# Self attention of a decoder kernel: low parts of the output weights and of the second half's key weights moved from VectorE to GpSimd

## The chip, the cores and the metric

One core of one Trainium2 chip runs the whole kernel. The metric is the device time of one execution in microseconds (us). The engines named below are TensorE (PE), VectorE (DVE), ScalarE (ACT), GpSimd (POOL) and SyncE (SP), which issues the DMAs.

## What is computed

The reference is a decoder of two layers over x of shape (16, 112, 512). Each layer is self attention, attention to a context, and a feed-forward part. The change touches only the second of these six parts, the attention of layer 0 with 16 query heads, 8 key heads and a head width of 128. It works on 16 sequences of 112 positions:

```python
b, s, _ = hidden_states.shape
ln_out = _ln(hidden_states, ln_w, ln_b)
q = _fp8_linear_pertensor(ln_out, wq, wq_scale, q_in_scale).reshape(b, s, g, hpg, d)
q = _ln(q, qln_w, qln_b)
k = _fp8_linear_pertensor(ln_out, wk, wk_scale, k_in_scale).reshape(b, s, g, d)
k = _ln(k, kln_w, kln_b)
v = _fp8_linear_pertensor(ln_out, wv, wv_scale, v_in_scale).reshape(b, s, g, d)
core = _gqa(q, k, v).reshape(b, s, nh * d)
...
cat = jnp.concatenate([core, xout], axis=-1)
catq = _div_clamp_fp8(cat, proj_smooth)
return jnp.einsum('bsi,oi->bso', catq, wproj) * (proj_in_scale * proj_w_scale)
```

The kernel keeps every weight matrix as the sum of two matrices of a reduced 32-bit format (fp32r): a high part, which is the scaled weight rounded, and a low part, which is the scaled weight minus the high part. A product with a weight is then two matmuls.

## The kernel before

`normed_attention` (L615) runs twice, once for self attention (`own` is true) and once for the context. Its work is cut into 32 steps (`STEPS`): 16 sequences for the first half of the heads (half 0, steps 0 to 15), then the same 16 for the second half (half 1, steps 16 to 31). Every eighth step (7, 15, 23, 31) is a "spread" step, whose sequence needs no query and key projection of its own. The output projection `project_out(b)` does nothing for b = 0, 8, 16, 24, and otherwise runs in step b+1.

Each engine has its own program, one written-out order per engine, and they meet at semaphores; the functions `step` in the five blocks set what stands ahead of what. In a step b of self attention:

- TensorE transposes the normalised queries and keys of b (`turn`, L960 and L965), projects the values (`unit(b, LU)`), does the scores (L1002), projects queries and keys of b+1 (`unit(b+1, 0)`, `1`, then `2`), transposes the probabilities (`turn_probs`, L1016), runs `project_out(b-1)` and weighs the values (L1030).
- ScalarE casts the input of b+1 (`cast`, L1100 and L1101), scales the transposed queries and keys (`take_turned`, L1136), takes the values (L1124), computes the exponentials (L1145) and copies the transposed probabilities (`take_probsT`, L1156).
- VectorE finds the maxima (`top`, L1254), inverts the sums and scales the probabilities (`probabilities`, L1266), measures and normalises the units of b+1 (L1232, L1239, L1248), adds the output (`add_out`, L1319), and scales and quantises the attention output (L1278 to L1289).
- GpSimd turns variances into reciprocal roots (`root`, L845 and L848), keeps rows for the spread step (L854, L856), moves a tail (`move_tail`, L883) and rounds the quantised output (`round_cat`, L860 to L870).

The weights of a half come in 16 pieces: four each for the queries (QS), keys (KS), values (VS) and outputs (OS). A query or output piece is 128x1024, a key or value piece is 128x512. For each piece SP loads the raw data (L576), ScalarE makes the high part (`round_high`, L591) and VectorE or GpSimd the low part (`low_by_dve`, L603; `low_by_pool`, L596). `on_dve` (L563) says which engine it is, and `wait_low` makes TensorE wait on the right semaphore. All pieces of self attention have a scale. VectorE applies it in the same instruction; GpSimd's form has no scale, so for its pieces ScalarE first scales the raw piece in place (`scale_raw`, L582). Before the change that was done for the output pieces of the context attention only.

The raw buffer of the output weights is loaded for half 1 by `replace_out(1, B - 1)`: SP waits for the last output projection of half 0, which is `project_out(15)` and runs in step 16, and then issues four loads of 512 KB. The output weights of a half are first used by `project_out(1)` in step 2 and by `project_out(17)` in step 18, and there each pair of heads waits for its own piece:

```python
if b % B == 1 and h % 2 == 0:
    weights.wait_low(pe, half_of(b), OS[h // 2:h // 2 + 1])
```

The keys of half 1 are first used by `unit(16, 2)` in step 15, which waits for the low part of all four pieces (`wait_low` takes the last one).

## Time and profile before

| | |
|---|---|
| median of three runs | 3477.82 us (3476.34 to 3480.4) |
| the profiled execution's own time | 3475.95 us |
| its span | 3474.2 us |
| TensorE busy | 3212.3 us, 92% |
| VectorE busy | 2367.2 us, 68% |
| ScalarE busy | 1666.6 us, 48% |
| GpSimd busy | 927.3 us, 27% |

Self attention of layer 0 takes the stretch from 244 us to 800 us of the span. Times in the rows below are microseconds from the start of the span. In a row of the timeline, the brackets at the end give how long the engine was idle before it and what released it. Where several instructions of a kind are merged, the duration is that of the whole run of them.

### The profile page before, as it was taken

The numbers are of one execution on the slowest core, as the hardware profiler recorded it, in microseconds if no ns is written. First come the engines' busy times: TensorE is split into PE (matmuls) and PEld (weight loads), VectorE is DVE, ScalarE is ACT, GpSimd is POOL, SyncE is SP. The second block draws the span as 40 slices with busy tenths as digits, with TensorE's granted clock in tenths as the row PEclk, the third lists the DMA queues.
The fourth block names the chain that finished last, engine by engine and source line by source line (L and its number), as shares of the span: only waits on it lengthen the run. The fifth ranks groups of instructions, "written<-read, shape, count | busy, mean of one in ns | idle before, by whom it ended". The sixth has DMA issues, their size and how long they took to land. (4 is left out here: it accounts for less than half of the span.)

```text
span 3474.2 us, 50564 instructions
## 1 busy us (share of the span) xinstructions
PE 3212.3 (92%) x17648; PEld 2611.9 (75%) x17648; DVE 2367.2 (68%) x6126; ACT 1666.6 (48%) x3735; POOL 927.3 (27%) x1073
## 2 busy tenths in 40 slices
PE   5758999998999999999999979999989879998999
PEld 4637777876787787777778757888868767776788
DVE  5988788786666666766666666999755555558433
ACT  4665454453433444544334433888447655542222
POOL 2544554552322222442223214000323310000000
PEclk9979999999999999999999989999999999999999
DMA  6130010011000001201101136999710134443000
GB/s 237 31 88 5 1 50 25 1 47 60 28 24 22 21 31 44 70 29 36 43 29 33 36 108 224 392 402 401 286 34 1 50 117 144 143 136 121 13 13 19
DMA packets 125229, 311.99 MB, mean 90 GB/s; under 512 B 42816, under 2 KB 46400, under 8 KB 119216
## 3 DMA queue, kind: packets, MB, share of 16 engines
q1 hardware_dynamic: 118816, 291.08, 23.8%
q0 software_dynamic: 6160, 17.67, 1.7%
q8 instruction: 143, 2.34, 0.3%
q14 instruction: 110, 0.90, 0.1%
HBM read 258.99 MB, written 49.02 MB: 89 GB/s over the span
## 5 line engine op out<-in xcount | busy, mean ns | idle before, releaser
L42 PE MATMUL bank<-w,cross_ctx_part 128*125 128x512 f32 x1536 | 516.8, 417 | 11.8 <-DVE cross_ctx_part L1225 9.0
L42 PEld LDWEIGHTS bank<-w,cross_ctx_part 128*125 128x125 f32 x1536 | 281.5, 186 | 96.6 <-DVE cross_ctx_part L1225 12.0
L1145 ACT ACTIVATE cross_prob<-bank,cross_neg_max 112x375 f32<-112x375 f32 x256 | 147.3, 575 | 338.9 <-DVE cross_neg_max L1254 337.5
L42 PE MATMUL bank<-w_low,cross_ctx_part 128*125 128x512 f32 x768 | 302.7, 394 | 0.0
L1254 DVE TENSOR_REDUCE cross_neg_max<-bank 112x1 f32<-112x375 f32 x256 | 134.3, 525 | 209.7 <-PE bank L1002 206.7
L42 PE MATMUL bank<-moe_wt,moe_zT 128*128 128x448 f32 x1176 | 263.3, 372 | 0.6 <-DVE moe_wt L1948 0.6
L1948 DVE TENSOR_TENSOR moe_wt<-moe_raw,moe_wt 128x1792 fp32r<-128x1792 f32 (+1 forms) x111 | 231.5, 2106 | 15.4 <-ACT moe_wt L1842 15.0
L42 PE MATMUL bank<-mlp_zT,mlp_signs 128*128 128x512 f32 (+1 forms) x1024 | 221.0, 369 | 6.2 <-DVE mlp_zT L2696 6.2
L42 PEld LDWEIGHTS bank<-moe_wt,moe_zT 128*128 128x128 f32 x1176 | 214.6, 189 | 15.8 <-DVE moe_wt L1948 0.8
L42 PE MATMUL bank<-w,self_xq 128*128 128x512 f32 (+1 forms) x464 | 194.0, 418 | 21.3 <-DVE w_low L603 19.9
L1842 ACT ACTIVATE moe_wt<-moe_raw 128x1792 fp32r<-128x1792 f32 (+1 forms) x111 | 196.8, 1775 | 29.2 <-DMA moe_raw<-in_moe_w 17.2
L42 PEld LDWEIGHTS bank<-mlp_zT,mlp_signs 128*128 128x128 f32 x1024 | 177.7, 189 | 43.4 <-issue 6.4
L42 PE MATMUL bank<-wo,full_tile 128*128 128x512 f32 x432 | 185.0, 428 | 10.5 <-POOL full_tile L867 7.3
L42 PE MATMUL bank<-w_low,self_xq 128*128 128x512 f32 (+1 forms) x464 | 185.6, 400 | 0.0
L1159 ACT ACTIVATE cross_probT<-bank 125x336 f32<-125x336 f32 x256 | 111.7, 447 | 145.8 <-PE bank L1016 145.7
L1248 DVE TENSOR_SCALAR cross_kn<-bank,cross_mv,cross_rstd 125x128 f32<-125x128 f32 x384 | 131.0, 403 | 71.2 <-POOL cross_rstd L848 71.1
L845 POOL TENSOR_TENSOR cross_ve<-cross_mv,eps 125x4 f32<-125x4 f32 (+1 forms) x152 | 30.9, 203 | 538.8 <-DVE cross_mv L1239 538.8
L1002 PE MATMUL bank<-cross_kT,cross_qT 128*112 128x375 f32 x448 | 173.8, 481 | 0.0
L42 PE MATMUL bank<-wo_low,full_tile 128*128 128x512 f32 x432 | 173.2, 401 | 0.0
L42 PEld LDWEIGHTS bank<-w_low,cross_ctx_part 128*125 128x125 f32 x768 | 142.5, 186 | 36.0
L1124 ACT ACTIVATE cross_v<-bank 125x512 f32<-125x512 f32 x96 | 57.4, 598 | 230.2 <-PE bank L1030 122.8
L1030 PE MATMUL bank<-cross_probT,cross_v 125*128 125x224 f32 x768 | 167.5, 354 | 0.0
(442 smaller groups left out, 7960.6 us busy)
## 6 DMA issues: line engine op xcount, KB each, us to landing
moe_raw<-in_moe_w SPq DMA_DIRECT2D x74, 896.0 KB, 7.4
moe_raw<-in_moe_w SPq DMA_DIRECT2D x37, 1024.0 KB, 8.1
stream<-in_L1f SPq DMA_DIRECT2D x32, 768.0 KB, 7.7
cross_ctx_raw<-in_ctxT SPq DMA_DIRECT2D x32, 750.0 KB, 4.4
wide_ctxT<-in_ctxT SPq DMA_DIRECT2D x16, 750.0 KB, 4.1
wide_ctx_rows<-in_ctx SPq DMA_DIRECT2D x16, 750.0 KB
expert_rows<-a_zeros SPq DMA_DIRECT2D x1, 8960.0 KB, 25.9
moe_zrow<-expert_rows SPq DMA_DIRECT2D x35, 256.0 KB, 7.7
```

The source lines that it names most:

```text
L42: mm = pe.matmul(out, a, b, start=first and n == 0, stop=last and n == len(pairs) - 1)
L845: pool.tensor_tensor(ve[0:rows, n, :], mv[0:rows, n, :, 1], k.eps[0:rows, 0:4], ALU.add)\
L1002: mm = pe.matmul(score_bank(t)[0:S, i * NK:(i + 1) * NK], queries[:, h, 0:S], keys[:, h // 2, 0:NK], start=True, stop=True)
L1030: mm = pe.matmul(ps[6 + pair // 2][:, at:at + 2 * S], v[:, j, pair * P:(pair + 1) * P], probsT_of(pair, j), start=j == 0, stop=j == KT - 1)
L1124: act.activation(v[:, j, :], unit_bank(b, LU + j)[0:KN, :], ACT.Copy).then_inc(s["v_ready"], 1)
L1145: op = act.activation(prob[:, t % SLOTS, i, :], score_bank(t)[0:S, i * NK:(i + 1) * NK], ACT.Exp, bias=neg_max[:, h:h + 1], accum_out=tota ...
L1159: act.activation(probT[:, (t // 2) % 2, :, t % 2, :], probs_bank(t)[0:KN, 0:KT * S].rearrange("p (j t) -> p j t", t=S), ACT.Copy).then_inc ...
L1248: op = dve.tensor_scalar(out, unit_bank(b, n)[0:rows, h * P:(h + 1) * P], mv[0:rows, n, h, 0:1], rstd[0:rows, n, h:h + 1], ALU.subtract, A ...
L1254: dve.tensor_reduce(neg_max[:, HS * t:HS * (t + 1)], score_bank(t)[0:S, 0:HS * NK].rearrange("p (h n) -> p h n", h=HS), AX.X, ALU.max, neg ...
L1842: act.activation(wt[:, PLACES[n % 4], 0, 0:w], raw[:, n % RAW, 0:w], ACT.Copy).then_inc(s["w_high"], 1)
L1948: dve.tensor_tensor(wt[:, PLACES[n % 4], 1, 0:w], raw[:, n % RAW, 0:w], wt[:, PLACES[n % 4], 0, 0:w].bitcast(F32), ALU.subtract).then_inc( ...
```

## The change

The low parts of all output pieces of self attention (half 0 and half 1) and of the key pieces of half 1 go to GpSimd, with a scaling in place on ScalarE ahead of each rounding. The places in the orders change too. In half h, counted from its first step (`at` is b modulo 16):

- Before, ScalarE rounded output pieces 0 and 1 at the end of step 0 (half 0) or 17 (half 1), and pieces 2 and 3 ahead of `cast_for_values` in step 1 or 18. VectorE made their low parts at the end of step 0 or 17 and after `normalise(b+1, 1)` in step 1 or 18.
- Now ScalarE scales and rounds piece 0 at the end of step `at` = 0, piece 1 between the two copies of the probabilities of `at` = 1, piece 2 at the end of `at` = 1, and piece 3 between the two copies of `at` = 2. GpSimd makes the low parts of pieces 0 and 1 after the last root of `at` = 1, piece 2 after the first root of `at` = 2 and piece 3 after the last root of `at` = 2.
- The four key pieces of half 1 are scaled in place and rounded at the end of step 14. GpSimd makes the low parts of three of them ahead of the first root of step 15 and that of the fourth ahead of the second root. Before, VectorE made two after the maxima of step 15 and two after the second `probabilities`.

```diff
     def on_dve(self, half, i):
-        return i in QS or half < 2 or (half == 2 and i not in OS)
+        return i in QS or (half < 3 and i in VS) or (half in (0, 2) and i in KS)
@@ GpSimd, step
+                    if own and g == B - 1:
+                        weights.low_by_pool(pool, half + 1, ((KS[0:3]), (KS[3:4]), ())[n])
                     if has(g + 1, n):
                         root(g + 1, n)
+                    if own and at == 1 and n == LU - 1:
+                        weights.low_by_pool(pool, half, OS[0:2])
+                    if own and at == 2 and n in (0, LU - 1):
+                        weights.low_by_pool(pool, half, OS[2:3] if n == 0 else OS[3:4])
@@ ScalarE, step
-                if own and b in (1, B + 2):
-                    weights.round_high(act, half, OS[2:4])
...
                     take_probsT(b, t)
+                    if own and at in (1, 2) and t == 0:
+                        weights.scale_raw(act, half, OS[2 * at - 1:2 * at])
+                        weights.round_high(act, half, OS[2 * at - 1:2 * at])
...
                     weights.round_high(act, half + 1, QS[3:4])
+                    if half + 1 == 1:
+                        weights.scale_raw(act, half + 1, KS)
                     weights.round_high(act, half + 1, KS)
-                if own and b in (0, B + 1):
-                    weights.round_high(act, half, OS[0:2])
+                if own and at in (0, 1):
+                    weights.scale_raw(act, half, OS[2 * at:2 * at + 1])
+                    weights.round_high(act, half, OS[2 * at:2 * at + 1])
@@ VectorE, step
-                if own and at == B - 1:
+                if own and b == STEPS - 1:
                     weights.low_by_dve(dve, half + 1, KS[0:2])
...
-                    if at == B - 1:
+                    if b == STEPS - 1:
                         weights.low_by_dve(dve, half + 1, KS[2:4])
...
-                    if b in (1, B + 2):
-                        weights.low_by_dve(dve, half, OS[2:4])
...
-                if own and b in (0, B + 1):
-                    weights.low_by_dve(dve, half, OS[0:2])
```

ScalarE's order from the end of step 16 to the start of step 18, before. L1156 copies transposed probabilities, L1100 and L1101 cast the next input, L1136 takes the transposed queries and keys of the next step:

```order
L1156 ACTIVATE self_probT<-bank 112x448 x2
L1100 ACTIVATE self_xq<-xq_self 128x8x112
L1101 ACTIVATE self_xq<-xq_self 128x8x16
L1136 ACTIVATE self_qT<-bank,head_ln 128x512 x2
L1136 ACTIVATE self_kT<-bank,head_ln 128x512
L1124 ACTIVATE self_v<-bank 112x512
```

The same place with the change (every line number above 900 is six higher):

```order
L1162 ACTIVATE self_probT<-bank 112x448 x2
L582 ACTIVATE wo_raw<-wo_raw,proj_scale 128x1024
L591 ACTIVATE wo<-wo_raw 128x1024
L1106 ACTIVATE self_xq<-xq_self 128x8x112
L1107 ACTIVATE self_xq<-xq_self 128x8x16
L1142 ACTIVATE self_qT<-bank,head_ln 128x512 x2
L1142 ACTIVATE self_kT<-bank,head_ln 128x512
```

Output piece 0 of half 1 now stands on ScalarE a whole step earlier, ahead of the cast for step 18 and of the queries and keys of step 17; before, nothing of the output weights stood in step 16.

GpSimd's order from the last root of step 17 into step 18, before (L845 and L848 are a root, L860 to L870 `round_cat`, L883 the tail):

```order
L848 TENSOR_TENSOR self_rstd<-self_ve,minus_half 128x4
L860 TENSOR_TENSOR self_scaled<-self_probT 128x896
L867 TENSOR_TENSOR full_tile<-self_scaled,self_probT 128x8x16
L870 TENSOR_TENSOR self_scaled<-self_scaled,self_probT 128x8x96
L854 COPY self_spread_room<-self_kT 128x4x16
L856 COPY self_spread_room<-self_qT 128x8x16
```

And with the change, to the end of step 18's roots (steps 1 and 2 of half 0 read the same):

```order
L596 TENSOR_TENSOR wo_low<-wo_raw,wo 128x1024 x2
L860 TENSOR_TENSOR self_scaled<-self_probT 128x896
...
L845 TENSOR_TENSOR self_ve<-self_mv,eps 128x4
L848 TENSOR_TENSOR self_rstd<-self_ve,minus_half 128x4
L596 TENSOR_TENSOR wo_low<-wo_raw,wo 128x1024
L845 TENSOR_TENSOR self_ve<-self_mv,eps 128x4
L848 TENSOR_TENSOR self_rstd<-self_ve,minus_half 128x4
L845 TENSOR_TENSOR self_ve<-self_mv,eps 128x4
L848 TENSOR_TENSOR self_rstd<-self_ve,minus_half 128x4
L596 TENSOR_TENSOR wo_low<-wo_raw,wo 128x1024
L883 CAST full_tile<-self_scaled 128x8x96
```

Two pieces stand ahead of `round_cat` of step 17, one between the first and the second root of step 18, and the last one behind the third root.

## Rows read from the trace of the kernel before

**Rows 1.** Page, groups: count, busy us, mean ns, idle before and releaser.

```profile
L42 PE MATMUL bank<-w,self_xq 128*128 128x512 f32 (+1 forms) x464 | 194.0, 418 | 21.3 <-DVE w_low L603 19.9
```

**Rows 2.** Timeline of PE: the scores of steps 9 and 10, undisturbed (start, duration).

```profile
414.12 1.73 PE L1002 MATMUL bank<-self_kT,self_qT 128*112 128x112 f32 x16
429.59 1.74 PE L1002 MATMUL bank<-self_kT,self_qT 128*112 128x112 f32 x16
```

**Rows 3.** Timeline of PE: the scores of steps 1 to 3, and 15 to 19.

```profile
281.37 1.73 PE L1002 MATMUL bank<-self_kT,self_qT 128*112 128x112 f32 x16
303.15 1.73 PE L1002 MATMUL bank<-self_kT,self_qT 128*112 128x112 f32 x16
319.46 1.73 PE L1002 MATMUL bank<-self_kT,self_qT 128*112 128x112 f32 x16
...
507.99 1.73 PE L1002 MATMUL bank<-self_spread_room 128*112 128x112 f32 x16
532.12 1.73 PE L1002 MATMUL bank<-self_kT,self_qT 128*112 128x112 f32 x16
548.44 1.73 PE L1002 MATMUL bank<-self_kT,self_qT 128*112 128x112 f32 x16
565.27 1.90 PE L1002 MATMUL bank<-self_kT,self_qT 128*112 128x112 f32 x16
587.46 1.73 PE L1002 MATMUL bank<-self_kT,self_qT 128*112 128x112 f32 x16
```

**Rows 4.** By tile wo_low: the low parts on DVE (ns min/median/max; first and last start).

```profile
L603 DVE SCALAR_TENSOR_TENSOR wo_low<-wo_raw,proj_scale,wo x8: 1262/1272/2924, 281.4 to 579.1; 128x1024 fp32r<-128x1024 f32 x8
```

**Rows 5.** The new instructions' kinds, by tile wo_low, wo_raw and w_low, in the context attention.

```profile
L596 POOL TENSOR_TENSOR wo_low<-wo_raw,wo x8: 2353/2386/2398, 859.7 to 1514.6; 128x1024 fp32r<-128x1024 f32 x8
L582 ACT ACTIVATE wo_raw<-wo_raw,proj_scale x8: 1138/1139/1143, 847.2 to 1474.4; 128x1024 f32<-128x1024 f32 x8
L596 POOL TENSOR_TENSOR w_low<-w_raw,w x8: 1254/1290/2749, 1409.6 to 1430.4; 128x512 fp32r<-128x512 f32 x8
```

**Rows 6.** Timeline of POOL and DVE in step 10, undisturbed: first and third root, one DVE product.

```profile
435.68 0.20 POOL L845 TENSOR_TENSOR self_ve<-self_mv,eps 128x4 f32<-128x4 f32 x1 [0.90 <-DVE self_mv L1239]
435.95 1.27 POOL L848 TENSOR_TENSOR self_rstd<-self_ve,minus_half 128x4 f32<-128x4 f32 x1
440.21 0.20 POOL L845 TENSOR_TENSOR self_ve<-self_mv,eps 128x4 f32<-128x4 f32 x1 [1.22 <-DVE self_mv L1239]
...
432.93 1.39 DVE L1266 TENSOR_TENSOR self_prob<-self_prob,self_inverse 112x448 f32<-112x448 f32 x1
```

**Rows 7.** Timeline of PE, steps 10, 15 and 18: transposed probabilities, waits for low parts.

```profile
437.10 0.55 PE L1016 MATMUL bank<-ident,self_prob 112*112 112x112 f32 x4
518.54 0.79 PE L42 MATMUL bank<-w,self_xq 128*128 128x512 f32 x1 [2.74 <-DVE w_low L603]
579.27 0.79 PE L42 MATMUL bank<-wo,full_tile 128*128 128x512 f32 x1 [2.68 <-DVE wo_low L603]
```

**Rows 8.** Windows behind such waits: busy us by PE, PEld, DVE, ACT, POOL; granted clock; DMA.

```profile
518.60:524.60 6.00, 6.00 (x17) 4.72 (x18) 4.58 (x26) 1.72 (x4) 2.71 (x5) 0.50 0.00 0
579.30:582.40 3.10, 3.10 (x7) 2.45 (x8) 1.11 (x1) 0.00 (x0) 0.00 (x0) 0.50 0.00 0
```

**Rows 9.** SP's issue of half 1's output weights, the first's time to landing, a window (columns as rows 8).

```profile
543.94 1.75 SPq L576 DMA_DIRECT2D wo_raw<-in_L0x_proj  x4
wo_raw<-in_L0x_proj SPq DMA_DIRECT2D x1, 512.0 KB, 3.7
540.60:548.10 7.50, 7.50 (x42) 6.45 (x41) 7.07 (x24) 3.30 (x6) 1.87 (x3) 1.00 0.41 128
```

**Rows 10.** Timeline of ACT, PE and POOL at the key weights of half 1.

```profile
516.27 2.55 ACT L591 ACTIVATE w<-w_raw,raw_scale 128x512 fp32r<-128x512 f32 x4
510.34 0.47 PE L42 MATMUL bank<-w,self_xq 128*128 128x512 f32 x1 [0.62 <-ACT self_v L1124]
513.79 0.87 POOL L870 TENSOR_TENSOR self_scaled<-self_scaled,self_probT 128x128 f32<-128x128 f32 x1
```

## The prediction

> **What bounds the kernel now.** I read the page first. TensorE is busy for 92% of the span, and its largest self-attention group has 21.3 us of idle time before it, 19.9 of them put down to VectorE's low parts at L603 [rows 1]. That is what a change of this kind can get at, so I went to the timeline of TensorE and took the distance between the scores of one step and of the next as the length of a step. A step that holds no output projection and is not disturbed lasts 15.47 us (step 9 to 10) [rows 2]; one that holds it lasts 16.31 us (step 2 to 3) [rows 3]. Against these the steps that handle weights are long: 1 to 2 takes 21.78 us, which is 6.3 too many; 15 to 16 takes 24.13, 7.8 too many; 17 to 18 takes 16.83, 1.4 too many; and 18 to 19 takes 22.19, 5.9 too many [rows 3]. Step 16 to 17, at 16.32 us, and step 2 to 3 lose nothing today. The reader is to see in these rows that 21.4 us are lost, and that two of the places which the change fills with new work are clean now. In this stretch a delay of TensorE's scores passes on to everything behind it: the undisturbed steps have the same length one after another, so no slack takes it up.
>
> **Step 1 to 2: the gain.** VectorE's low parts take 1.27 us each and up to 2.92 us [rows 4]. Two at the end of step 0 hold up the maxima of step 1, and two more stand ahead of the keys of step 2. All four leave. ScalarE's work of 2.3 us between the two copies of the probabilities delays the second copy by some 0.5 us, but in the undisturbed step TensorE waits there for the queries anyway. So the step goes to 15.5 us: **-6.3** (bounds -6.3 and -5).
>
> **Step 2 to 3: a new wait.** One output piece costs GpSimd 2.39 us [rows 5]. I count from the start of the step's first root, T, which is 435.68 in the undisturbed step; the third root starts at T+4.5, and the second transposition of probabilities starts at T+1.4, some 0.35 us ahead of the output projection, which so begins at T+1.75 [rows 6, 7]. A root is two instructions, 0.2 and 1.0 to 1.3 us. With the change the first root ends at T+1.55, piece 2 at T+4.0, the second root at T+5.3, the third, which no longer can start at T+4.5, at T+6.6, and piece 3 at T+9.1. TensorE takes 0.93 us for each pair of heads (four matmuls 0.23 us apart), so it wants piece 2 at T+3.6 and piece 3 at T+4.9 with the first wait in it. It waits 0.4 and 4.2, together 4.6 us. A wait of this length has so far been followed by half clock: behind the waits of 2.74 and 2.68 us the granted clock is 0.50, which is 1.2 GHz, for 6.0 and 3.1 us [rows 7, 8], and half of that time is lost, 3.0 and 1.6 us. I take 1.6, since most of what follows in the step is short.
>
> There is one more term. Pieces 0 and 1 start behind the third root of step 1 and take 4.8 us, while VectorE quantises the output (L1284 to L1289) and GpSimd's `round_cat` stands behind them. Where both engines work from SBUF, instructions of one form stretch: VectorE's L603 from 1.27 to 2.92 us [rows 4], GpSimd's L596 for a key piece from 1.29 to 2.75 [rows 5], and VectorE's product L1266 takes 1.39 us in step 10, where `round_cat` is running on GpSimd [rows 6]. I read these as waits of one engine for the other's instruction to end. If VectorE's quantising waits for a piece in that way, the maxima of step 2 come 1.5 us late, of which about 0.5 is slack. I take **1.0** (bounds 0.3 and 1.8). So step 2 to 3 becomes 16.3 + 1.0 + 4.6 + 1.6 = 23.5 us: **+7.2** (bounds +5 and +10). Half 0 as a whole comes out at +0.9.
>
> The Trainium skill (GPSIMD Engine Reference, Key points) says that GpSimd shares its SBUF interfaces with VectorE and contends with VectorE's instructions in a two-port mode or with two SBUF inputs. L1266 and L603 have two SBUF inputs, and the trace agrees, with 1.39 and 2.92 us; that the quantising instructions would be held by their two-port mode is the page's word alone, and by it the term would stand at its upper bound. The same page (Engine selection) says that an elementwise operation of two inputs is about twice as slow on GpSimd as on VectorE, which speaks against this move; here it is 2.39 us [rows 5] against 1.27 [rows 4].
>
> **Step 15 to 16: the keys.** ScalarE scales four 128x512 pieces in place at the end of step 14, at about 0.63 us each by the high parts' 2.55 for four [rows 10]: 2.5 us more ahead of the cast and of the values of step 15. TensorE waits for those values today (0.62 us at 510.34 [rows 10]), since `unit(16, 0)` uses their bank, so this is paid in full. GpSimd is through with `round_cat` at 514.7 [rows 10], and by some 0.7 us earlier without VectorE's low parts beside it; three pieces at 1.29 us [rows 5], a root of 1.3 and the fourth piece end at 520.5 without a clash and at 521.5 with VectorE's two products between them. TensorE gets past that wait at 518.54 today [rows 7]. The loss is 2.0 to 3.0 us; VectorE's relief in this step doesn't help, because the keys' low parts are what ends last. I take **+3.0**, with the queue behind it (the second root of step 16 also comes later) (bounds +1.5 and +4.5).
>
> **Step 16 to 17: ScalarE waits for a load.** SP issues the four loads of the output weights of half 1 at 543.94, when the last output projection of half 0 is done, and the first lands 3.7 us later, at 547.6 [rows 9]. The change puts piece 0 at the end of ScalarE's step 16, ahead of everything of step 17, and ScalarE gets there before the load is even issued. It stands until 547.6, scales and rounds until 549.9 (1.14 [rows 5] and nearly as much again), and then has the cast and the taking of queries and keys to do, 3.3 us of work that today lies between 540.6 and 548.1 [rows 9]; so the keys are ready at 553.2. Today the scores start at 548.44 [rows 3]. **+4.8** (bounds +4.2 and +6).
>
> **Step 17 to 18.** The low parts of output pieces 0 and 1 stand at the end of VectorE's step 17 and hold up step 18, not this one; its excess of 1.4 us today I read as a stretch of half clock (the scores at 565.27 take 1.90 us and not 1.73 [rows 3]). The wait of 4.8 us would bring half clock too, for 1.6 to 3 us of loss. 15.5 + 1.6 = 17.1: **+0.3** (bounds -1.4 and +1.6).
>
> **Step 18 to 19.** The same walk as for step 2 to 3 gives 23.5 against 22.19 today, which already holds VectorE's two delays: **+1.3** (bounds -1 and +4).
>
> **The sum.** -6.3 + 7.2 + 3.0 + 4.8 + 0.3 + 1.3 = +10.3 us. Against the profiled execution's own 3475.95 us that gives 3486.3; the median of the runs is 1.87 above that execution, so the forecast is **3488 us**, 0.3% slower. With all lower bounds together the sum is +3, with all upper ones +25. The rest of the kernel is shifted, not changed: its loads and pieces of half 2 and 3 stand as before. What the change takes from VectorE, eight low parts of output pieces [rows 4] and four of half the size, is some 13 us of work, of which only the two places above ended anything.
>
> **The rivals.** *VectorE was what ended these steps, and its relief counts* (faster). For it: 19.9 us of TensorE's idle time are booked on L603 [rows 1]. The mechanism would be that GpSimd's last output piece is in time and the key pieces end no later than now. Then half 0 gives -6.3, step 18 to 19 -5.9, the keys 0, ScalarE's wait +4.8: -7.4, or 3470 us. It decides if piece 3 ends before T+4.9; against it is the order, which puts it behind the third root at T+4.5, so that it cannot end before T+6.9.
>
> *The new waits are short* (about the same). Piece 3's wait is as long as today's 2.68, nothing clashes (0.3), the keys cost 1.5: -6.3 + 4.6 + 1.5 + 4.2 + 0 - 1.3 = +2.7, or 3480.5 us.
>
> *The clashes chain and the clock stays low* (slower than forecast). Each of the three waits of over 4 us is followed by 3 us of loss instead of 1.6, and VectorE is held by each of GpSimd's pieces: +18 or more, 3496 us.
>
> *The change doesn't do what it says* is out: the order of the instructions has eight output and four key pieces on GpSimd and none of them on VectorE in self attention.
>
> **How the numbers follow.** Forecast 0.66, same 0.18, worse chain 0.08, faster 0.08. A difference of 0.2%, 7 us, is about what a measurement of this kernel can tell from none; the forecast's own spread reaches below +7 in some part, which I put at 0.08 of its 0.66. So faster 0.08, within 0.2% 0.25, slower 0.67. The range of 3477 to 3496 holds the forecast, nearly all of the "same" case and the near part of the worse one.
>
> **What would show it.** In the profile after: ScalarE idle before L582 at 541 to 547 us, released by a DMA; TensorE's scores of step 17 waiting for ScalarE's L1142 by nearly 5 us; TensorE waiting for GpSimd's L596 ahead of the last pair of heads in steps 2 and 18, by 4 us; step 1 to 2 at 15.5 us; TensorE waiting for GpSimd in step 15. If the waits on L596 are under 2 us, or the scores of step 17 are on time, the prediction is wrong.

## The result, and the profile after

The changed kernel takes 3490.17 us in the median of seven runs (3488.74 to 3493.9), the kernel before, on the same chip, 3479.21 us (3476.09 to 3482.69). The ratio is 1.0029, with a 95% interval of 1.002 to 1.0038: slower, by 10 to 11 us. Forecast were 3488 us and a loss of 10.3 us.

The profiled execution of after, at 3493.9 us, is the longest of its seven, and its span is 17.7 us above that of before. Part of that lies outside self attention. From the scores of step 0 to those of step 31 the distance is 515.09 us before and 525.42 us after, 10.3 us more, and that is what the rest of this section is about. The page of after:

```profile
span 3491.9 us, 50588 instructions
PE 3222.2 (92%) x17648; PEld 2619.0 (75%) x17648; DVE 2354.9 (67%) x6114; ACT 1676.7 (48%) x3747; POOL 946.7 (27%) x1085
...
L42 PE MATMUL bank<-w,self_xq 128*128 128x512 f32 (+1 forms) x464 | 195.2, 421 | 23.3 <-DVE w_low L603 17.2
...
L42 PE MATMUL bank<-wo,full_tile 128*128 128x512 f32 x432 | 183.3, 424 | 15.5 <-POOL wo_low L596 8.2
```

Twelve instructions have left VectorE and twelve have come to ScalarE and to GpSimd, as the diff says. TensorE's idle time ahead of the projections has not become less (23.3 us against 21.3 in [rows 1]), and of the 15.5 us ahead of the output projections (10.5 before) 8.2 are now a wait for GpSimd's low parts.

Windows of after, each from one step's scores to the next one's: steps 0 to 3, then 15 to 19 (busy us of PE, PEld, DVE, ACT, POOL; granted clock; share and rate of the DMA):

```profile
264.69:285.15 20.46, 18.14 (x84) 14.63 (x85) 13.33 (x51) 10.10 (x27) 4.86 (x8) 0.85 0.00 1
285.15:303.36 18.21, 15.28 (x78) 12.26 (x77) 15.47 (x51) 12.29 (x29) 12.53 (x12) 0.85 0.00 1
303.36:325.61 22.25, 18.93 (x93) 15.89 (x92) 13.89 (x52) 10.09 (x27) 14.86 (x15) 0.89 0.00 0
514.14:540.19 26.05, 20.06 (x94) 16.23 (x93) 18.07 (x58) 14.10 (x36) 15.35 (x14) 0.87 0.13 41
540.19:561.22 21.03, 16.49 (x93) 13.79 (x92) 14.20 (x52) 10.26 (x28) 12.29 (x12) 0.99 0.28 101
561.22:577.46 16.24, 14.84 (x77) 12.36 (x77) 12.81 (x48) 12.01 (x29) 8.23 (x10) 0.90 0.01 2
577.46:601.60 24.14, 19.23 (x94) 15.51 (x93) 15.74 (x54) 9.98 (x27) 15.81 (x16) 0.86 0.00 0
```

Against the starts in [rows 3]:

| step | before | after | difference | forecast |
|---|---|---|---|---|
| 0 to 1 | 18.95 | 20.46 | +1.5 | none |
| 1 to 2 | 21.78 | 18.21 | -3.6 | -6.3 |
| 2 to 3 | 16.31 | 22.25 | +5.9 | +7.2 |
| 15 to 16 | 24.13 | 26.05 | +1.9 | +3.0 |
| 16 to 17 | 16.32 | 21.03 | +4.7 | +4.8 |
| 17 to 18 | 16.83 | 16.24 | -0.6 | +0.3 |
| 18 to 19 | 22.19 | 24.14 | +1.9 | +1.3 |
| 22 to 23 | 14.71 | 13.15 | -1.6 | none |

The steps 0 to 1 and 22 to 23 hold none of the moved waits. They differ with the time at which stretches of half clock fall, and so they do between all kernels of this study (18.95 to 20.52, and 13.15 to 14.71); together they cancel here. Steps with work of their own vary in the same way: 2 to 3 lasts from 22.2 us to 24.06 (keys_back, where the granted clock of the step is 0.84 and not 0.89) in kernels that don't differ there. So a difference of up to 1.8 us in a single step needs a look at the clock first. All other steps agree within 0.1 us or so.

TensorE's timeline after, at the places the prediction speaks of (the brackets: idle time and what ended it):

```profile
297.52 0.66 PE L966 MATMUL bank<-ident,self_qn 128*128 128x128 f32 x4 [1.84 <-DVE self_qn L1258]
303.36 2.48 PE L1008 MATMUL bank<-self_kT,self_qT 128*112 128x112 f32 x16
318.27 0.57 PE L42 MATMUL bank<-wo,full_tile 128*128 128x512 f32 x1 [3.32 <-POOL wo_low L596]
518.56 0.47 PE L42 MATMUL bank<-w,self_xq 128*128 128x512 f32 x1 [2.69 <-ACT self_v L1130]
527.06 0.79 PE L42 MATMUL bank<-w,self_xq 128*128 128x512 f32 x1 [2.61 <-POOL w_low L596]
561.22 2.02 PE L1008 MATMUL bank<-self_kT,self_qT 128*112 128x112 f32 x9 [4.54 <-ACT self_kT L1142]
588.74 0.50 PE L42 MATMUL bank<-wo,full_tile 128*128 128x512 f32 x1 [1.31 <-POOL wo_low L596]
593.54 0.79 PE L42 MATMUL bank<-wo,full_tile 128*128 128x512 f32 x1 [3.60 <-POOL wo_low L596]
```

Each forecast wait is there: for GpSimd ahead of the last pair of heads (3.32 and 3.60 us), for ScalarE's keys at step 17 (4.54), for the values and GpSimd's key pieces in step 15. ScalarE's timeline shows where the 4.54 come from:

```profile
555.83 1.15 ACT L582 ACTIVATE wo_raw<-wo_raw,proj_scale 128x1024 f32<-128x1024 f32 x1 [7.00 <-DMA wo_raw<-in_L0x_proj]
557.07 1.06 ACT L591 ACTIVATE wo<-wo_raw 128x1024 fp32r<-128x1024 f32 x1
558.03 0.93 ACT L1106 ACTIVATE self_xq<-xq_self 128x896 fp32r<-128x896 bf16 x1
559.07 1.43 ACT L1142 ACTIVATE self_qT<-bank,head_ln 128x512 f32<-128x512 f32 x2
560.39 0.77 ACT L1142 ACTIVATE self_kT<-bank,head_ln 128x512 f32<-128x512 f32 x1
```

It stands 7.0 us for the load, then scales and rounds, and casts the input and takes queries and keys only then. GpSimd's timeline in step 2, each root by its first instruction alone: the first root and piece 2 at 309.49 to 313.4, two roots, and piece 3 last, until 318.2:

```profile
309.49 0.20 POOL L845 TENSOR_TENSOR self_ve<-self_mv,eps 128x4 f32<-128x4 f32 x1 [0.90 <-DVE self_mv L1249]
311.02 2.39 POOL L596 TENSOR_TENSOR wo_low<-wo_raw,wo 128x1024 fp32r<-128x1024 f32 x1
313.38 0.19 POOL L845 TENSOR_TENSOR self_ve<-self_mv,eps 128x4 f32<-128x4 f32 x1
314.63 0.20 POOL L845 TENSOR_TENSOR self_ve<-self_mv,eps 128x4 f32<-128x4 f32 x1
315.88 2.34 POOL L596 TENSOR_TENSOR wo_low<-wo_raw,wo 128x1024 fp32r<-128x1024 f32 x1
```

So the sum came out, but not all of its terms. My theory for the runs: the loss has three places, the load that ScalarE waits for, GpSimd's last output piece, and the keys. The rivals: that GpSimd's clashes with VectorE or the stretches of half clock make it, or that ScalarE's scaling in place does.

### The profile page after: what moved, and what is told of

Its sections match the earlier page's. It is cut to its first block and busy times, and to the rows that moved or that the text cites. A ratio compares the mean times of both kernels' runs of the same rounds, so it can differ in the third digit from the quotient of the medians.

```text
span 3491.9 us, 50588 instructions
## 1 busy us (share of the span) xinstructions
PE 3222.2 (92%) x17648; PEld 2619.0 (75%) x17648; DVE 2354.9 (67%) x6114; ACT 1676.7 (48%) x3747; POOL 946.7 (27%) x1085
## 5 line engine op out<-in xcount | busy, mean ns | idle before, releaser
L42 PEld LDWEIGHTS bank<-moe_wt,moe_zT 128*128 128x128 f32 x1176 | 213.4, 188 | 15.6 <-DVE moe_wt L1954 0.8
L42 PE MATMUL bank<-w,self_xq 128*128 128x512 f32 (+1 forms) x464 | 195.2, 421 | 23.3 <-DVE w_low L603 17.2
L42 PE MATMUL bank<-wo,full_tile 128*128 128x512 f32 x432 | 183.3, 424 | 15.5 <-POOL wo_low L596 8.2
L845 POOL TENSOR_TENSOR cross_ve<-cross_mv,eps 125x4 f32<-125x4 f32 (+1 forms) x152 | 30.7, 202 | 538.6 <-DVE cross_mv L1249 538.6
```

The costliest lines, as they stand in the source:

```text
L42: mm = pe.matmul(out, a, b, start=first and n == 0, stop=last and n == len(pairs) - 1)
```

## The experiments

Four kernels each take one thing out of the changed one. They ran on one chip, on which before took 3488.91 us (22 runs); another chip took 3480.52 (25 runs) for the same program, so only ratios are compared across chips, and the steps of the traces say more than totals.

**keys_back.** VectorE makes the low parts of the keys of half 1 again, as before, and ScalarE doesn't scale them.

```
 def on_dve(self, half, i):
-    return i in QS or (half < 3 and i in VS) or (half in (0, 2) and i in KS)
+    return i in QS or (half < 3 and i not in OS)
...
-if own and g == B - 1:
-    weights.low_by_pool(pool, half + 1, ((KS[0:3]), (KS[3:4]), ())[n])
...
-if half + 1 == 1:
-    weights.scale_raw(act, half + 1, KS)
...
```

> The changed kernel with the key pieces of half 1 back on VectorE, unscaled by ScalarE, as before the change. Theory (each new place in the orders has its own wait): step 15 to 16 falls from 26.1 us to 24.1, the 2.7 us wait of TensorE for the values goes, the total falls by 2 us and by no more. Rival (VectorE's relief in step 15 is worth something and the loss lies elsewhere): step 15 to 16 stays at 26 us or grows.

3497.75 us (3494.49 to 3504.32), ratio 1.0033 (1.0019 to 1.0047). Step 15 to 16 takes 23.55 us, 2.5 less than in after; 16 to 17 and 18 to 19 stay at 20.97 and 24.14. From the scores of step 0 to those of 31 it takes 522.57 us, 2.9 less than after, which a total of this spread doesn't show: the ratio to before is no smaller than that of after, 1.0029. The window of step 15:

```profile
511.67:535.22 23.55, 18.55 (x93) 14.96 (x92) 22.23 (x62) 12.13 (x32) 12.07 (x10) 0.93 0.13 45
```

TensorE waits 0.71 us for the values there (2.69 in after) and 2.74 for VectorE's key pieces, which it passes 10.6 us behind the scores, as in before. VectorE is busy for 22.23 us of the step and not for 18.07, and the step is shorter: its relief there buys nothing.

**load_wait.** In half 1 alone each output piece's scaling and rounding stands one place later on ScalarE, so piece 0 comes in the middle of step 17, behind the keys.

```
 if own and at in (1, 2) and t == 0:
-    weights.scale_raw(act, half, OS[2 * at - 1:2 * at])
+    i = 2 * at - 1 - half
+    weights.scale_raw(act, half, OS[i:i + 1])
...
-if own and at in (0, 1):
+if own and at in (half, half + 1):
+    i = 2 * at - half
```

> The changed kernel with ScalarE's four output pieces of half 1 each one place later (middle and end of step 17, middle and end of step 18), so that none stands at the end of step 16; GpSimd's places stay. Theory: ScalarE's idle time of 7.0 us before L582 goes, step 16 to 17 falls from 21.0 us to 16.3, the total by 4.7 us; step 18 to 19 stays within 1 us of 24.1. Rival (ScalarE's extra scaling costs, wherever it stands): step 16 to 17 falls, but 17 to 18 and 18 to 19 take it back, and the total moves by less than 2 us.

3490.97 us (3484.62 to 3497.47), ratio 1.0007 (0.9996 to 1.0019), where after had 1.0029. Windows of steps 16 to 17, 17 to 18, 18 to 19:

```profile
539.87:556.20 16.33, 16.33 (x94) 13.96 (x92) 14.14 (x52) 8.10 (x25) 8.54 (x10) 1.00 0.22 69
556.20:571.65 15.45, 13.27 (x78) 10.85 (x77) 13.28 (x49) 12.17 (x29) 12.35 (x12) 1.00 0.16 65
571.65:595.11 23.46, 18.54 (x94) 15.06 (x93) 15.63 (x54) 12.07 (x29) 15.69 (x16) 0.85 0.00 0
```

The step has its length of before again, 16.33, TensorE is busy in all of it, and the one behind it is undisturbed at 15.45 and full clock. The wait for the load is worth 4.7 us there and 0.8 in the next step, which it left at a clock of 0.90. Step 18 to 19 is 0.7 us shorter too, though GpSimd's last piece ends 16.0 us behind the scores in both; that is within what the clock moves. Self attention goes from 525.42 to 519.25 us.

**last_wait.** In steps 2 and 18 the product of the last output piece (heads 6 and 7) with its low part is left out, and TensorE waits for it one step later. All of GpSimd's work stays.

```
+late = own and b % B == 1 and h >= 6
-if b % B == 1 and h % 2 == 0:
+if b % B == 1 and h % 2 == 0 and not late:
     weights.wait_low(pe, half_of(b), OS[h // 2:h // 2 + 1])
+if late and h == 6:
+    pe.wait_ge(k.piece_high, weights.every.index((half_of(b), OS[3])) + 1)
+if own and b % B == 2 and h == 6:
+    weights.wait_low(pe, half_of(b), OS[3:4])
...
-             [part[:, h, :] for part in wo_parts], h == 0, h == H - 1)
+             [part[:, h, :] for part in (wo_parts[:1] if late else wo_parts)], h == 0, h == H - 1)
```

> The changed kernel in which the output projections of steps 2 and 18 leave out the low product of the last output piece (heads 6 and 7), so that TensorE waits for that piece only one step later. Two matmuls fewer per place are 0.5 us. Theory (GpSimd's last piece comes too late): the waits on L596 in steps 2 and 18 fall from 3.3 and 3.6 us to under 0.5, the half clock behind them goes, step 2 to 3 falls from 22.3 us to about 17.5 and 18 to 19 from 24.1 to about 19, the total by 9 to 11 us. Rival (contention of GpSimd and VectorE in these steps): the two steps fall by 1 us each at most, since all of GpSimd's work stays.

3486.68 us (3482.97 to 3490.41), ratio 0.9995 (0.9986 to 1.0005). Windows of steps 2 to 3 and 18 to 19, and the wait left in the first:

```profile
299.70:317.85 18.15, 16.37 (x91) 13.40 (x90) 14.22 (x52) 10.09 (x27) 15.02 (x15) 1.00 0.00 0
569.57:587.68 18.11, 16.35 (x92) 13.40 (x92) 14.20 (x51) 10.09 (x27) 15.00 (x15) 1.00 0.00 0
...
310.97 0.50 PE L42 MATMUL bank<-wo,full_tile 128*128 128x512 f32 x1 [1.32 <-POOL wo_low L596]
```

18.15 and 18.11 us against 22.25 and 24.14, and no half clock in either: piece 3's wait and the clock behind it cost 4.1 and 6.0 us (the two products left out, 0.23 us each, are in that). What remains of both above 16.31 is the wait of 1.32 for piece 2, for which the expectation had under 0.5, and half a microsecond. Self attention takes 512.25 us, 13.2 less than after, for 9 to 11 expected; 3 of that lie outside the two steps, mostly in steps 0 to 2 and 15 to 16, where the clock was better. This is the largest place of the three.

**no_scaling.** ScalarE's scaling in place is left out for both halves of self attention, and the high parts are rounded without a scale; all else stays.

```
 for i in which:
+    if half < 2:
+        continue
     raw = piece_of(*self.raw, i)
...
+if half < 2 and (half, i) in self.by_pool:
+    scale = None
...
```

> The changed kernel without the scaling in place on ScalarE for the pieces of self attention that GpSimd handles; the weights of those pieces stay unscaled in both parts. Twelve ScalarE instructions go, 8 of 1.14 us and 4 of 0.63. Theory: only where ScalarE's piece ends a wait does it matter: 1.2 us in step 16 to 17 and 1 to 2.5 us in step 15 to 16, the total falls by 2 to 4 us. Rival (the extra ScalarE work is the main cost): the total falls by 9 us or more.

3497.5 us (3491.19 to 3503.96), ratio 1.0034 (1.0019 to 1.0049). Windows of steps 15 to 16 and 16 to 17, and TensorE's one wait of length in step 15:

```profile
512.30:538.35 26.05, 18.69 (x93) 15.03 (x92) 18.87 (x58) 11.78 (x32) 15.32 (x14) 0.87 0.12 41
538.35:558.12 19.77, 16.50 (x93) 13.78 (x91) 14.19 (x52) 9.10 (x27) 11.77 (x12) 1.00 0.30 107
...
525.19 0.80 PE L42 MATMUL bank<-w,self_xq 128*128 128x512 f32 x1 [6.25 <-POOL w_low L600]
```

Step 16 to 17 falls by 1.26, a little over one scaling (1.15). But step 15 to 16 stays at 26.05 us to the hundredth: the wait for the values, 2.69 in after, is gone, and the wait for GpSimd's key pieces has grown from 2.61 to 6.25. GpSimd ends the keys, 12.9 us behind the scores in both, whatever ScalarE does before. The expectation missed here: it had 1 to 2.5 us for this step and 2 to 4 for the whole, and self attention takes 524.94 us, 0.5 less than after. The rival, 9 us or more, is out.

The next four ran on a second chip (before 3480.52 us, 25 runs).

**mix.** Takes all three places away and keeps the use of GpSimd where there is room: the keys as in keys_back; output pieces 0 and 1 by GpSimd, from scaled raws; pieces 2 and 3 by VectorE, one behind the maxima of step 2 and one behind the first queries' normalising; ScalarE takes up half 1's pieces only in the middle of step 17. Its edit against the changed kernel, cut:

```
 def on_dve(self, half, i):
-    return i in QS or (half < 3 and i in VS) or (half in (0, 2) and i in KS)
+    return i in QS or (half < 2 and i in OS[2:4]) or (half < 3 and i not in OS)
...
-if own and at == 2 and n in (0, LU - 1):
-    weights.low_by_pool(pool, half, OS[2:3] if n == 0 else OS[3:4])
...
 top(b, 1)
+if own and at == 2:
+    weights.low_by_dve(dve, half, OS[2:3])
...
 normalise(b + 1, 0)
+if at == 2:
+    weights.low_by_dve(dve, half, OS[3:4])
```

> Keys of half 1 on VectorE as before the change. Of the output pieces, 0 and 1 by GpSimd after the last root of steps 1 and 17, as in the change, and 2 and 3 by VectorE in steps 2 and 18: piece 2 right behind the maxima, piece 3 behind the first normalisation, where the walk gives VectorE slack. ScalarE has no output piece in step 16. Theory (only pieces that are late where they are wanted, or ahead of work that is wanted, cost): steps 1 to 2, 2 to 3 and 18 to 19 take 15.5 to 18, 17 to 18 and 17 to 19 us, step 16 to 17 takes 16.3; self attention from the first scores to the last is 506 to 510 us against 515.1 of the kernel before and 525.4 of the change, and the kernel is 5 to 9 us faster than before. Rival (VectorE's low parts or the clashes with GpSimd cost wherever they stand): 515 us or more.

3474.1 us (3470.81 to 3484.93), ratio 0.998 (0.9967 to 0.9993). From scores 0 to scores 31 it takes 507.85 us, 7.2 less than before. Windows of steps 1 to 2, 2 to 3 and 18 to 19:

```profile
281.74:299.37 17.63, 14.69 (x77) 11.70 (x76) 14.94 (x50) 11.23 (x28) 12.53 (x12) 0.91 0.01 1
299.37:317.14 17.77, 16.95 (x93) 14.04 (x92) 16.39 (x55) 9.24 (x26) 10.41 (x12) 0.99 0.00 0
562.97:580.63 17.66, 16.82 (x94) 13.89 (x92) 16.26 (x55) 9.25 (x26) 10.40 (x12) 1.00 0.00 0
```

**slots.** The kernel before, with output pieces 2 and 3 put on VectorE at the two places of mix, and nothing given to GpSimd. ScalarE rounds them later too, at the end of steps 1 and 17 and in the middle of steps 2 and 18.

```
-if own and b in (1, B + 2):
-    weights.round_high(act, half, OS[2:4])
+if own and at == 2 and t == 0:
+    weights.round_high(act, half, OS[3:4])
...
+if own and at == 2:
+    weights.low_by_dve(dve, half, OS[2:3])
...
-if b in (1, B + 2):
-    weights.low_by_dve(dve, half, OS[2:4])
```

> The kernel before the change, nothing on GpSimd: output pieces 2 and 3 moved on VectorE to the two places of the kernel above, pieces 0 and 1 left at the end of steps 0 and 17. Theory: the two late pieces cost nothing there, but pieces 0 and 1 still hold up the maxima: steps 1 to 2 and 18 to 19 keep 2 to 4 us of their excess of 6, and self attention takes 508 to 512 us. If GpSimd's share is what brings the gain, it stays at 514 to 516.

3475.1 us (3472.54 to 3479.92), ratio 0.9989 (0.9977 to 1.0). Windows of steps 1 to 2 and 18 to 19:

```profile
283.07:302.48 19.41, 14.95 (x78) 11.58 (x76) 16.82 (x53) 9.13 (x26) 11.15 (x11) 0.92 0.00 1
565.57:584.55 18.98, 17.11 (x93) 13.88 (x92) 18.70 (x54) 9.24 (x26) 11.13 (x12) 1.00 0.00 0
```

Its total in self attention is 512.08 us, 3.0 less than before, at the edge of what was expected. But its step 0 to 1, which no edit touches, lasted 20.51 us for 18.95, by its stretch of half clock (a granted clock of 0.85 for 0.93); in the steps that the edits do touch slots gains 4.5 us and mix 7.0. So well over half of mix's gain needs no GpSimd, and some 2.5 us are what GpSimd and ScalarE take over. That last part rests on one trace of each kernel: the medians, 3475.1 and 3474.1 us, don't tell the two apart, and the interval of slots reaches 1.0.

**piece3_early.** In the changed kernel both of GpSimd's pieces of step 2 stand ahead of its later roots.

```
-if own and at == 2 and n in (0, LU - 1):
-    weights.low_by_pool(pool, half, OS[2:3] if n == 0 else OS[3:4])
+if own and at == 2 and n == 0:
+    weights.low_by_pool(pool, half, OS[2:4])
```

> The changed kernel with GpSimd's last output piece right behind the third one, ahead of the second and third roots of steps 2 and 18. Theory (the wait is set by the place in GpSimd's queue): TensorE's wait for the last piece falls by 2.3 us, but the later roots and with them the queries and keys come 2.4 us later, so that the two steps fall by 0.5 to 2.5 us each. Rival (contention sets it): the wait moves by less than 1 us.

One run, 3486.76 us. Its window of step 2 to 3 and TensorE's wait in step 18:

```profile
300.34:320.41 20.07, 17.48 (x94) 14.07 (x92) 15.39 (x54) 10.20 (x27) 14.08 (x14) 0.98 0.00 0
...
585.65 0.50 PE L42 MATMUL bank<-wo,full_tile 128*128 128x512 f32 x1 [1.12 <-POOL wo_low L596]
```

20.07 and 20.46 us for the two steps, 2.2 and 3.7 less than in after (0.5 to 2.5 were expected), but 1.9 and 2.3 more than without the wait for piece 3. With the two pieces ahead, GpSimd's second root starts at 313.43, 6.2 us behind the first one, for 3.9 in after (309.49 and 313.38), and TensorE then waits 0.94 us for the next keys (318.05). Neither of the two orders serves both, but this one is the better: self attention takes 518.86 us, 6.6 less than after, part of it by the clock.

**after_again.** The changed kernel unchanged, beside the others.

> The changed kernel itself, beside the others on the same chip. Self attention takes 524 to 527 us from the first scores to the last, with the steps 2 to 3, 15 to 16, 16 to 17 and 18 to 19 at 22.3, 26, 21 and 24 us within 1 us (the clock's phase moves them); the total is 10 to 11 us above the kernel before.

3488.65 us (3485.03 to 3491.66), ratio 1.0027 (1.0016 to 1.0038): the first comparison again on another chip. Self attention takes 525.13 us, as expected; the total is 8.1 us above before, for 10 to 11 expected.

The last two ran on a third chip (before 3481.56 us, 10 runs).

**quarters.** Tests the clash. GpSimd's output pieces 0 and 1 are cut into four instructions of 256 columns each.

```
+parts = 4 if half < 2 and i in OS[0:2] else 1
...
+for n in range(parts):
+    part = slice(n * size, (n + 1) * size)
+    op = pool.tensor_tensor(low[:, part], raw[:, part], high[:, part], ALU.subtract)
```

> The changed kernel with each of GpSimd's low parts of output pieces 0 and 1 cut into four instructions of 256 columns. Theory (VectorE's quantising waits for one GpSimd instruction to end, but that wait is hidden behind the scores of the next step): VectorE's first quantising instruction in steps 1 and 17, 2.63 us in the change against 0.63 undisturbed, falls to 1.3 or less, and no step gets shorter by more than 0.4 us. Rival (the exclusion costs 1 us per half, as the prediction's sum had it): steps 2 to 3 and 18 to 19 fall by 1 us each.

One run, 3490.06 us. VectorE's first quantising instruction, first in after (steps 1 and 17), where GpSimd works on a piece, then in quarters (step 1):

```profile
300.07 2.63 DVE L1294 TENSOR_SCALAR self_probT<-self_scaled 128x896 bf16<-128x896 f32 x1
576.14 2.67 DVE L1294 TENSOR_SCALAR self_probT<-self_scaled 128x896 bf16<-128x896 f32 x1
```

```profile
298.12 0.75 DVE L1299 TENSOR_SCALAR self_probT<-self_scaled 128x896 bf16<-128x896 f32 x1
```

In the kernel before, where GpSimd is idle in step 10, it takes 0.63 us:

```profile
428.27 0.63 DVE L1284 TENSOR_SCALAR self_probT<-self_scaled 128x896 bf16<-128x896 f32 x1
```

So the hold of 2 us is real, and cutting the pieces removes it from VectorE. No step gets shorter by it: 2 to 3 takes 23.22 us (22.25 in after) and 18 to 19 24.72 (24.14), and where 1 to 2 is shorter, with 16.24, it ran at a better clock. Self attention takes 525.67 us, the same as after.

But GpSimd gains no time by the cutting. Its rows in step 17, first in quarters, then in after:

```profile
572.47 6.25 POOL L601 TENSOR_TENSOR wo_low<-wo_raw,wo 128x256 fp32r<-128x256 f32 x8
...
573.61 4.72 POOL L596 TENSOR_TENSOR wo_low<-wo_raw,wo 128x1024 fp32r<-128x1024 f32 x2
579.75 1.90 POOL L860 TENSOR_TENSOR self_scaled<-self_probT 128x896 f32<-128x896 bf16 x1 [1.42 <-DVE self_probT L1299]
585.05 0.20 POOL L845 TENSOR_TENSOR self_ve<-self_mv,eps 128x4 f32<-128x4 f32 x1
```

In after GpSimd itself waits 1.42 us for the quantising that its own piece held up. Its first root of step 18 starts 7.6 us behind the scores (577.46), for 6.1 in step 10 (435.68 behind 429.59), and from there to the end of piece 3 it is never idle. In quarters that wait is gone, but the eight cut instructions take 6.25 us where the two whole ones take 4.72 (the shortest of the eight takes 0.72 us, so most of that is their number), and the first root of step 18 starts 7.6 us behind the scores as well (583.87 behind 576.32). So quarters leaves GpSimd as late as it was, and doesn't show what the clash costs.

**mix_keys.** mix, with two of half 1's key pieces on GpSimd (scaled by ScalarE) and two on VectorE.

```
-if own and at == B - 1:
-    weights.low_by_dve(dve, half + 1, KS[0:2])
+if own and at == B - 1:
+    weights.low_by_dve(dve, half + 1, KS[0:2] if half else KS[2:4])
...
+if own and g == B - 1 and n == 0:
+    weights.low_by_pool(pool, half + 1, KS[0:2])
```

> The mixed kernel (output pieces 0 and 1 by GpSimd, 2 and 3 by VectorE) with the keys of half 1 shared too: pieces 0 and 1 by GpSimd, scaled in place by ScalarE, ahead of the first root of step 15, and pieces 2 and 3 by VectorE behind the maxima. Theory (the keys' loss is set by what ends last, two pieces on each engine end at the same time): step 15 to 16 falls from 24.0 to 21.5 to 23.5 us, and self attention from 507.9 us to 505 to 507.5. Rival (ScalarE's two scalings ahead of the values of step 15 give it back): 24 us or more.

3472.83 us (3470.16 to 3476.06), ratio 0.9972 (0.9961 to 0.9984), the lowest ratio of the study. Its window of step 15 to 16 and the wait in it:

```profile
506.49:528.55 22.06, 17.14 (x94) 13.96 (x92) 21.75 (x60) 13.07 (x34) 14.50 (x12) 1.00 0.14 48
...
516.04 0.50 PE L42 MATMUL bank<-w,self_xq 128*128 128x512 f32 x1 [1.76 <-POOL w_low L596]
```

The step takes 22.06 us against 24.13 before and 23.95 in mix: with the pieces on both engines the last one ends earlier than with either alone, 9.6 us behind the scores for 10.6 with VectorE and 12.9 with GpSimd. Self attention takes 507.31 us, 0.5 less than mix: steps that don't differ between the two move by up to 1.6 us each with the clock, and together take most of the 1.9 us back. Mix and mix_keys are not told apart by their totals.

## Why the prediction came out right

The direction, the size and the range held; 3488 was forecast and 3490.17 came, with the ratio 1.0029 for a forecast of 1.003. Two of the three losses are right in their mechanism, the load and the late last piece; the third, the keys, is a real loss that was put down to the wrong wait. That the sum meets the measured 10.3 us to the tenth is luck. (The prediction's sums of its bounds are off: its lower ones add up to +2.0 and not +3, its upper ones to +21.1 and not +25. The range doesn't hang on them.) By its own steps:

- **Step 16 to 17, the load: right.** +4.7 for +4.8, by the mechanism named, and load_wait takes exactly this back. The load released ScalarE 15.6 us behind the scores of step 16 (555.83), where the walk from [rows 9] had 15.5.
- **Step 2 to 3, the new wait: right in kind, two of its terms off.** In step 2 one wait of 3.32 us came for 0.4 and 4.2. TensorE was itself 0.75 us late there, since the scores took 2.48 us at half clock and not 1.73, and piece 3 ended 8.7 us behind the first root's start, for 9.1 forecast. In step 18, at full clock, they were 1.31 and 3.60, together 4.9, with GpSimd 1.5 us later than forecast (see the clash). The clock took 1.7 and 2.4 us for the 1.6: from the start of the last pair of heads to the next scores it is 7.3 and 8.1 us, and 5.6 in step 2 of before. With 0.75 for the slow scores, 3.5 for the wait (from where the last pair would have started) and 1.7 behind it, step 2 to 3 has its +5.9.
- **The clash: real, but not by the path of the sum.** The sum had VectorE's quantising held, the maxima of step 2 late by it, and 1.0 us lost in step 2 to 3; that the quantising would be held was left to a page. The hold came, and longer than the 1.5 us I had worked with (2.63 us for 0.63). The Trainium skill (GPSIMD Engine Reference, Key points) says that a two-port instruction of VectorE contends with GpSimd, without a time for it; the lengthening in the trace agrees, though no run here shows which mode the instruction is in. By the maxima nothing is lost: in step 2 VectorE waits another 1.52 us for TensorE's scores before them (305.08), and in step 18, where they end 0.9 us late, the second transposition of probabilities still starts 7.5 us behind the scores, as in step 10. What the sum overlooked is GpSimd's own queue, which waits for the held quantising: in step 18 the roots and pieces 2 and 3 come 1.5 us later by it (quarters). Up to 1.5 of TensorE's 4.9 us of waits there are the clash's, by my estimate from these rows. In step 2 of after the scores were late themselves by half clock, the first root started 6.1 us behind them as in step 10, and the term was nothing. No run has the step without a clash, so this price is argued and not shown.
- **Step 1 to 2: the gain was oversized, and this is the step that failed.** 18.21 us came for 15.5. I took the step without VectorE's four pieces to be undisturbed. It isn't: GpSimd stood 2.38 us in step 1 for nothing that the trace names, ahead of the copy of rows, with the clearing of past semaphores standing there in its program:

```profile
291.64 0.24 POOL L854 COPY self_spread_room<-self_kT 128x64 f32<-128x64 f32 x1 [2.38 <-issue]
```

  The roots, the queries and the scores come some 0.8 us later by that (TensorE waits 1.84 us for the queries where it waits 1.47 in an undisturbed step). last_wait and quarters show the step without half clock at 16.25 and 16.24 us, and this 0.8 is all that is left over 15.45. GpSimd's two pieces and ScalarE's work between the two copies are not it: load_wait has the same in step 17, without the standing, and that step lasts 15.45 us. In before GpSimd stood there too, 1.52 us, behind VectorE's lateness. The other 2.0 us of the 18.21 are half clock, from 298.3 to 304.4, for which the forecast of this step had no term; before had some as well, so that not all of its 6.3 us of excess were VectorE's:

```profile
281.37:303.15 21.78, 15.04 (x77) 12.06 (x76) 19.12 (x55) 10.17 (x27) 11.38 (x11) 0.92 0.00 1
```

  That GpSimd's standing is the clearing of semaphores is read from the program's order; no run took it out. So the best gain here is -5.5, and with the clock that fell it was -3.6.
- **Step 15 to 16, the keys: right in sign, wrong in cause.** +1.9 for +3.0. I added ScalarE's 2.5 us "paid in full" to the step. That wait came (2.69 at 518.56, for 0.62), but no_scaling shows that it costs nothing, for GpSimd's pieces end last, at 527.0, 12.9 us behind the scores, which in before passed the wait 10.6 behind them. The lower of my two bounds, 2.0 from GpSimd's end, was the right account.
- **Steps 17 to 18 and 18 to 19:** -0.6 and +1.9 for +0.3 and +1.3, within their bounds. In 18 to 19 the waits were 4.9 us for 4.6 and the clock behind them cost 2.4 for 1.6.

The sum of +10.3 is met because these misses cancel: 2.7 us of gain less in step 1 to 2, against 1.3 less in step 2 to 3, 1.1 less in the keys, 0.9 less in step 17 to 18, with 0.6 more in step 18 to 19 and nothing left by the two uncounted steps. The mechanisms of the three losses are shown by the runs: taken away one at a time they give 2.9, 6.2 and 13.2 us of self attention (the last with a better clock in steps 0 to 2), and without all three the move is a gain (mix).

The rival "VectorE's relief counts" is not empty: in half 0 its gain is there, and slots shows that well over half of mix's gain needs no GpSimd at all. The rival of chained clashes, +18 us or more, didn't come: the stretches behind the waits of steps 2 and 18 cost 1.7 and 2.4 us and not 3 each, and beside the output pieces one quantising instruction is held in each half and not one for each piece. A part of it is there, though, in GpSimd's 1.4 us of step 18.

## What to carry to other kernels

Before moving work to an emptier engine, walk the queue of the engine that receives it and of the one that prepares it, up to the consumer's deadline: here GpSimd is busy for 27% of the span, and its last piece was still 3.3 and 3.6 us late. A step placed ahead of others on an in-order engine may wait only for what has landed by then; ScalarE's 2 us of work cost 4.7 us because its load had not. And a stretch that one late engine hides is not undisturbed once that engine is relieved: look for the next late instruction in it, and don't take another step's length for it. Where an engine holds up another, look whether it then waits for that one itself.

## What was not expected of the hardware

- A GpSimd subtraction of 2.39 us held one VectorE instruction, which reads one SBUF operand and takes 0.63 us alone, so that it took 2.63 and 2.67 us in steps 1 and 17. With GpSimd's instruction cut in four it took 0.75 us. In step 17 the hold lasts for what is left of GpSimd's: the pieces end at 578.33, the quantising at 578.81. The cut pieces took 6.25 us together, the whole ones 4.72.
- The key pieces on GpSimd took 1.27 to 1.69 us each beside VectorE, 4.55 for three where 3.87 was the sum without a clash [rows 5]; this is small beside the 2.75 that the row allowed.
- After waits of 3.3 and 3.6 us TensorE was granted 0.54 and 0.50 of its clock (its 1.2 GHz level) for the 3.0 and 3.6 us behind them; after the wait of 1.32 us in last_wait it stayed at 1.00. But the length of the wait alone doesn't settle it: in step 1 TensorE waits 1.84 us for the queries in after (297.52) and 1.85 in last_wait, and in after 6.1 us at 0.50 follow (298.3 to 304.4), in last_wait none (the window 283.45 to 299.70 is at 1.00). Where such stretches fall moved untouched steps by up to 1.6 us between kernels that don't differ there. The stretches behind the waits of steps 2 and 18 in after:

```profile
318.30:321.30 3.00, 3.00 (x8) 2.53 (x9) 1.13 (x3) 0.00 (x0) 0.82 (x1) 0.54 0.00 0
593.60:597.20 3.60, 3.60 (x9) 3.07 (x10) 1.55 (x4) 0.00 (x0) 0.82 (x1) 0.50 0.00 0
```

- The same program had medians of 3479.21, 3480.52, 3481.56 and 3488.91 us in four sets of runs: 0.3% between chips, as much as the whole effect of the change.
